# Waits of TensorE attached to other matmuls, fold and projection directly behind the pair sums, gathers one step further ahead

## The chip, the cores and the metric

The kernel runs on one core of one Trainium2 chip. The metric is device time in microseconds (us), here the median of three runs. TensorE multiplies matrices and writes to PSUM; VectorE, ScalarE and GpSimd work on elements (GpSimd on SBUF alone); each has its own queue, and the queues meet only at semaphores. In the profile PE is TensorE's matmul, PEld its weight load, DVE is VectorE, ACT ScalarE, POOL GpSimd and SP the queue that starts plain DMAs.

## The reference

Sixteen embedding tables are looked up for 2048 samples, which gives `e` of 16 fields by 256. Three layers of a field interaction follow, each with a weight of 16 by 256, then a small network of three matrices:

```python
    e = jnp.stack([tbl_0[ids[:, 0]], ...], axis=1)          # (2048, 16, 256)
    for i in range(n_layers):                                # 3
        z = jnp.einsum('bfe,bge->bfge', x, xk).reshape(B_, F_ * F_, E_)
        z = jnp.swapaxes(z, 1, 2)
        z = jnp.einsum('bcl,oc->bol', z, Ws[i]) + bs[i][None, :, None]
        z = jax.nn.relu(z)
        z = jnp.sum(z, axis=-1)
        outs.append(z)
        xk = jnp.broadcast_to(z[:, :, None], (B_, F_, E_))
    ...
    h = jnp.concatenate([z, dense_ctx], axis=1)              # 48 + 16
    h = jnp.maximum(h @ W_top1 + b_top1, 0.0)
    h = jnp.maximum(h @ W_top2 + b_top2, 0.0)
    y = h @ W_top3
```

Layer 0 multiplies every pair of fields element by element. In layers 1 and 2 the second factor is the same number over all elements, so the kernel projects `e` once and multiplies by it.

## The kernel before

**Tiling.** Eight samples of sixteen fields fill the 128 partitions. Two such tiles are one step; there are 128 steps (`STEPS`), and eight steps make a group `g` of 128 samples (16 groups). All engines walk through *slots* 0 to 159. In slot k each engine does its part of step k, or of a step a little ahead, and whatever piece of layers 1 and 2 or of the network the constants at the top put there (`ROUNDS`, `FOLD`, `PROJ`, and so on, as offsets to 8g).

**A step.** GpSimd gathers the rows of step k (two indirect DMAs, L257, into a ring `emb` of `EMB_RING` = 6), `LEAD` + 1 steps ahead of the product that it then makes. TensorE *transposes* them in slot k-2 (`turn`, L483, four matmuls with 128x128 weights into one of two halves of `turn_ps`). ScalarE copies them to `emb_t` (L398, L399). VectorE (L217), GpSimd (L217 and L267) and ScalarE (squares, L406) multiply the pairs into `prods`, a ring of three. TensorE then *sums the pairs* (`sum_pairs`, L503): 16 matmuls, in which four column strips of the array, 128 rows by 32 columns each, work side by side; they appear as 32 in the trace, since each f32 matmul is two passes. They go to the single buffer `sum_ps`, which ScalarE reads (`relu_pairs`, L416 and L419) before the next step's sums may start.

**Layers 1 and 2.** A *projection* (`project`, L546) per group, also with 128x32 strips. *Rounds* (`outer_round`, L531 and L535), four per layer and group, with 32x128 strips, into the single buffer `outer_ps`, which ScalarE reads (L426). There is one in slots 14 to 17, in every slot from 22 to 141, and in 146 to 149. A *fold* (`fold`, L555) per layer and group, with 128x32 strips again, which sums over one field: in slots 8g+18 and 8g+30. Projection, folds and both hidden layers (`hidden1` L563, `hidden2` L572) share the single buffer `wide_ps`; `wait_wide` waits for the reader of the one before. Small matmuls (`side`: L514, L517, L521) share a bank with the sums; `wait_side` waits for their readers.

**Order.** It is written out by hand. TensorE's loop over slots is `turn(slot + 2)`, a side matmul, `sum_pairs(slot)`, a round, and last the wide piece (projection, fold or hidden layer). GpSimd's loop, from slot -1, is a gather, `half_shift(slot + 1)`, a gather, `last_blocks(slot + 1)`, after `2 * LEAD` gathers in a row. An instruction holds one wait; further ones stand as separate waiting instructions before it in the queue. On TensorE the wait is on the weight load, and all waits of a block stand before its first matmul.

## Time and profile before

| | us |
|---|---|
| median of three runs | 630.85 (630.07 to 631.62) |
| profiled execution, whole | 628.34 |
| its span | 626.6 |
| TensorE busy (matmul) | 575.6 (92%) |
| VectorE busy | 499.5 (80%) |
| GpSimd busy | 463.7 (74%) |
| ScalarE busy | 455.3 (73%) |

The span runs from the first instruction to the last. Matmul times overlap, since one starts while the one before still drains, so the text measures TensorE from the start of one block to the start of the next. Slots 0 to 127 carry sums and end near 562 us; the rest of the span is the tail, in which only rounds, folds, hidden layers and small matmuls are left. The granted clock is the share of TensorE's 2.4 GHz that the chip gave; 0.50 is 1.2 GHz.

### The profile page before, as it was taken

The page shows a single profiled execution, that of the slowest core. Times are in us where ns is not written, and L with a number is a line of the kernel's source. Part 1 is how long each engine was busy: PE and PEld are TensorE (multiplying, and loading weights), DVE is VectorE, ACT ScalarE, POOL GpSimd, SP SyncE. Part 2 cuts the span into 40 slices and gives each one's busy share as a digit, 9 for nine tenths or more (in the row PEclk, how much of TensorE's full clock was granted, in tenths as well). Part 3 has the DMA queues.
Part 4 walks back from the last instruction along what each step waited for, and adds up shares of the span by engine and source line. Part 5 has one row for each costly group of instructions (what it writes and reads, how often), then busy time and mean ns, then how long its engine had stood idle before and what let it go on. Part 6 is the DMA issues. An engine that isn't in the chain of part 4 may idle for free.

```text
span 626.6 us, 19391 instructions
## 1 busy us (share of the span) xinstructions
PE 575.6 (92%) x7936; PEld 328.8 (52%) x7936; DVE 499.5 (80%) x220; ACT 455.3 (73%) x1298; POOL 463.7 (74%) x565
## 2 busy tenths in 40 slices
PE   2878798999999999999999999999999999997776
PEld 1444454555646555564656555565556555554354
DVE  5999999999898988889898988889888888941000
ACT  2666777787878787877887787777878788765542
POOL 6999999999988788888888888788878787621000
PEclk9999999999999999999999999999999999999988
DMA  3322222222222212222212122212212222100000
GB/s 97 112 73 73 69 70 68 70 70 65 69 64 61 61 58 63 61 61 62 65 56 65 57 61 60 69 55 68 60 55 67 61 61 57 47 3 1 1 1 2
DMA packets 14794, 35.97 MB, mean 57 GB/s; under 512 B 5922, under 2 KB 6306, under 8 KB 14690
## 3 DMA queue, kind: packets, MB, share of 16 engines
q0 software_dynamic: 12288, 33.57, 18.8%
q1 hardware_dynamic: 2418, 1.16, 0.7%
q8 instruction: 64, 1.05, 0.7%
q14 instruction: 24, 0.19, 0.1%
HBM read 34.70 MB, written 0.01 MB: 55 GB/s over the span
## 4 chain that ended last, share of the span: by engine, by line
PE 82%; POOL 8%; issue 4%; ACT 3%; DMA 1%; DVE 1%; SPq 0%; POOLq 0%
PE sum_ps L503 35%; PE turn_ps L483 10%; PE wide_ps L555 10%; PE outer_ps L535 8%; PE wide_ps L572 6%; PE wide_ps L546 4%; POOL emb L257 4%; PE outer_ps L531 4%; PE wide_ps L563 3%; POOL prods L267 2%; POOL prods L217 2%; ACT relu_k L426 1%; PE sum_ps L521 1%; PE sum_ps L517 1%; DVE prods L217 1%
## 5 line engine op out<-in xcount | busy, mean ns | idle before, releaser
L217 DVE TENSOR_TENSOR prods<-turn_ps,emb_t 128x3360 f32<-128x3360 f32 x128 | 466.1, 3655 | 55.1 <-ACT emb_t L399 52.2
L257 POOL DMA_INDIRECT emb<-tables,rows_sb x256 | 252.2, 985 | 45.4 <-issue 34.5
L503 PE MATMUL sum_ps<-prods,w_sb 128*32 128x272 f32 x4096 | 265.0, 397 | 18.6 <-POOL prods L217 11.1
L503 PEld LDWEIGHTS sum_ps<-prods,w_sb 128*32 128x32 f32 x4096 | 136.4, 110 | 103.6 <-issue 39.6
L426 ACT ACTIVATE relu_k<-outer_ps 128x1024 f32<-128x1024 f32 x128 | 132.4, 1035 | 11.2 <-PE outer_ps L535 11.1
L416 ACT ACTIVATE relu<-sum_ps,bias_sb 128x120 f32<-128x120 f32 x256 | 90.6, 361 | 58.4 <-PE sum_ps L503 57.2
L267 POOL TENSOR_TENSOR prods<-emb_t 128x256 f32<-128x256 f32 x128 | 95.3, 745 | 46.3 <-ACT emb_t L399 45.1
L398 ACT COPY emb_t<-turn_ps 128x512 f32<-128x512 f32 x128 | 75.3, 589 | 71.3 <-PE turn_ps L483 71.3
L483 PE MATMUL turn_ps<-ident_sb,emb 128*128 128x128 f32 x512 | 84.6, 289 | 12.7 <-DMA emb<-tables,rows_sb 10.0
L483 PEld LDWEIGHTS turn_ps<-ident_sb,emb 128*128 128x128 f32 x512 | 55.1, 142 | 60.5 <-issue 57.6
L406 ACT ACTIVATE prods<-emb_t 128x512 f32<-128x512 f32 x128 | 81.5, 637 | 3.3
L217 POOL TENSOR_TENSOR prods<-emb_t 128x224 f32<-128x224 f32 x128 | 77.5, 605 | 2.3
L535 PE MATMUL outer_ps<-proj_b,z_wide 32*128 32x256 f32 x1024 | 78.0, 378 | 0.0
L555 PE MATMUL wide_ps<-relu_k,fold_sb 128*32 128x256 f32 x1024 | 61.9, 382 | 1.5 <-ACT h L453 1.4
L291 POOL TENSOR_TENSOR z_wide<-z_cat,sample_sb 128x512 f32<-128x512 f32 x32 | 33.7, 1052 | 29.0 <-PE outer_ps L535 21.1
L369 DVE TENSOR_REDUCE z_cat<-wide_ps 128x16 f32<-128x256 f32 x32 | 13.4, 419 | 50.3 <-PE wide_ps L555 50.3
L416 ACT ACTIVATION_READ_ACCUMULATOR relu<-sum_ps,bias_sb 128x1 f32 x256 | 51.5, 201 | 0.0
L399 ACT COPY emb_t<-turn_ps 128x256 f32<-128x256 f32 x128 | 49.5, 386 | 0.0
L531 PE MATMUL outer_ps<-bias_wide,ones_sb 32*128 32x256 bf16 x512 | 37.0, 279 | 10.7 <-ACT relu_k L426 10.5
L531 PEld LDWEIGHTS outer_ps<-bias_wide,ones_sb 32*128 32x128 bf16 x512 | 12.9, 91 | 64.0 <-issue 52.7
L555 PEld LDWEIGHTS wide_ps<-relu_k,fold_sb 128*32 128x32 f32 x1024 | 30.3, 109 | 28.1 <-issue 9.3
L535 PEld LDWEIGHTS outer_ps<-proj_b,z_wide 32*128 32x128 f32 x1024 | 40.2, 186 | 0.0
(41 smaller groups left out, 284.3 us busy)
## 6 DMA issues: line engine op xcount, KB each, us to landing
emb<-tables,rows_sb POOLq DMA_INDIRECT x256
w_sb<-w_top SPq DMA_DIRECT2D x1, 512.0 KB, 4.3
ids_sb<-ids_t SPq DMA_DIRECT2D x1, 128.0 KB, 2.1
h<-dense_t SPq DMA_DIRECT2D x1, 128.0 KB, 2.9
w_sb<-w_top SPq DMA_DIRECT2D x1, 128.0 KB, 3.1
ident_sb<-ident SPq DMA_DIRECT2D x1, 64.0 KB, 2.1
w_sb<-w_cols SPq DMA_DIRECT2D x1, 64.0 KB, 1.9
wp_sb<-w_proj SPq DMA_DIRECT2D x1, 32.0 KB
```

Of the source, the lines that this page charges most:

```text
L217: eng.tensor_tensor(out, every, shifted, ALU.mult).then_inc(done, 1)
L257: nc.gpsimd.indirect_dma_start(out=emb[:, k % EMB_RING, t * E:(t + 1) * E], out_offset=None, in_=tables, in_offset=bass.IndirectOffsetOnAx ...
L267: nc.gpsimd.tensor_tensor(prod_blocks(k)[:, :, SHIFTS * F:], x[:, :, 0:SHIFTS], x[:, :, SHIFTS:F], ALU.mult).then_inc(prods_pool, 1)
L398: nc.scalar.copy(out[:, :, 0:F], src).then_inc(emb_t_ready, 1)
L406: nc.scalar.square(prod_blocks(k)[:, :, 0:F], emb_blocks(k)[:, :, 0:F]).then_inc(squares_ready, 1)
L416: nc.scalar.activation(relu0[:, t, :], sum_ps[:, t * PAIRS + F:(t + 1) * PAIRS], ACT.Relu, bias=bias_sb[:, 0:1], accum_out=pair_sum[:, g % ...
L426: nc.scalar.activation(relu_k[:, k, q, :, :], outer_ps[:, :, 0:F * F], ACT.Relu).then_inc(outer_relu, 1)
L483: last = nc.tensor.transpose(turn_ps[:, k % 2, i * P:(i + 1) * P], emb[:, k % EMB_RING, i * P:(i + 1) * P], ident_sb[:])
L503: last = nc.tensor.matmul(sum_ps[s * 2 * F:(s + 1) * 2 * F, 0:SUM_COLS], w_sb[:, c, odd, :], x[:, c, 2 * s + odd, :, :], start=c == 0 and ...
L531: nc.tensor.matmul(outer_ps[:, j, 0:F * F], ones_sb[j * R:(j + 1) * R, :], bias_wide[j * R:(j + 1) * R, k, :], start=True, stop=False)
L535: last = nc.tensor.matmul(outer_ps[:, j, 0:F * F], z_wide[j * R:(j + 1) * R, k, q, :], y[j * R:(j + 1) * R, k, :, :], start=False, stop=True)
L555: last = nc.tensor.matmul(wide_ps[j * R:(j + 1) * R, 0:F * F], fold_sb[:], relu_k[:, k, q, j, :], start=q == 0, stop=q == G4 - 1)
```

## The change

It does six things.

- `EMB_RING` goes from 6 to 8 and `LEAD` from 3 to 4: eight gathers stand before GpSimd's loop in place of six.
- The semaphores `prods_pool` and `squares_ready` are replaced by one per buffer of `prods` (`prods_other`, three increments per use), so that the sums wait for one.
- TensorE's waits go to other matmuls. The wait for a step's gather moves from its transposition into the sums of three steps before; the wait for ScalarE's reading of the sums goes to the fourth transposition of the slot, the one for a side matmul's reader to the third; `wait_wide` goes to the last of the 16 sums; the first round of four has its three waits on three matmuls. The wait for `emb_t_ready` in `turn` and that for `prods_dve` in the sums are left out, and so are the waits ahead of a side matmul for the readers of its bank, as the transpositions' waits stand before them.
- Projection and folds stand directly behind the sums, ahead of the slot's round. Hidden layers stay behind it.
- The last two steps (`STEPS - 2` on), which have no transposition beside them, keep their waits in front.
- ScalarE's `take_turned` waits for `sums_done` in place of two semaphores of products.

```diff
-EMB_RING = 6
+EMB_RING = 8
...
-LEAD = 3
+LEAD = 4
...
-        prods_pool = sem("prods_pool")
-        squares_ready = sem("squares_ready")
+        prods_other = [sem(f"prods_other{j}") for j in range(PRODS_RING)]
...
-                    at_least(act, prods_dve, old + 1)
-                    at_least(act, prods_pool, 2 * (old + 1))
+                    at_least(act, sums_done, old + 1)
...
             def turn(k):
 
                 if k < STEPS:
-                    pe.wait_ge(gathered[k % EMB_RING], PAIR * 16 * (k // EMB_RING + 1))
-                    at_least(pe, emb_t_ready, 2 * (k - 1))
+                    if k < 2:
+                        wait_gathered(k)
                     at_least(pe, prods_dve, k - 1)
                     for i in range(PAIR * EC):
+                        if i == 2 and k - 3 in SIDE_AT:
+                            wait_side(pe, k - 3)
+                        if i == 3:
+                            wait_sums_read(k - 2)
...
             def sum_pairs(k):
 
                 if k < STEPS:
-                    pe.wait_ge(squares_ready, k + 1)
-                    pe.wait_ge(prods_dve, k + 1)
-                    pe.wait_ge(prods_pool, 2 * (k + 1))
-                    wait_sums_read(k)
-                    wait_side(pe, k - 1)
+                    if k >= STEPS - 2:
+                        pe.wait_ge(prods_dve, k + 1)
+                        wait_side(pe, k - 1)
+                        wait_sums_read(k)
+                    pe.wait_ge(prods_other[k % PRODS_RING], N_OTHER * (k // PRODS_RING + 1))
...
+                                if (c, odd, s) == (1, 1, 2):
+                                    wait_gathered(k + 3)
+                                if (c, odd, s) == (1, 1, 3) and k in WIDE_AT and WIDE_AT[k][0] != "hidden2":
+                                    wait_wide(pe, *WIDE_AT[k])
...
             def outer_round(k, g, q):
 
-                if q == 0:
-                    pe.wait_ge(z_wide_ready[k], g + 1)
-                    pe.wait_ge(proj_ready, g + 1)
                 at_least(pe, outer_relu, ROUND_NO[k, g, q])
                 for j in range(J):
+                    if q == 0 and j == 1:
+                        pe.wait_ge(proj_ready, g + 1)
+                    if q == 0 and j == 2:
+                        pe.wait_ge(z_wide_ready[k], g + 1)
...
                 sum_pairs(slot)
+                if slot >= STEPS and slot in WIDE_AT:
+                    wait_wide(pe, *WIDE_AT[slot])
+                by_32 = slot in WIDE_AT and WIDE_AT[slot][0] in ("proj", "fold0", "fold1")
+                if by_32:
+                    wide(*WIDE_AT[slot])
                 if slot in ROUND_AT:
                     outer_round(*ROUND_AT[slot])
-                if slot in WIDE_AT:
+                if slot in WIDE_AT and not by_32:
                     wide(*WIDE_AT[slot])
```

TensorE in slot 30, before: L503 are the sums, L531 and L535 the round, L555 the fold, L483 the next transpositions.

```order
L503 MATMUL sum_ps<-prods,w_sb 32x272 [waits relu0_ready,prods_pool,z0_taken,prods_dve,squares_ready]
L503 MATMUL sum_ps<-prods,w_sb 32x272 x15
L531 MATMUL outer_ps<-bias_wide,ones_sb 128x256 [waits outer_relu,proj_ready,z_wide_ready0]
L531 MATMUL outer_ps<-bias_wide,ones_sb 128x256 x3
L535 MATMUL outer_ps<-proj_b,z_wide 128x256 x4
L555 MATMUL wide_ps<-relu_k,fold_sb 32x256 [waits outer_relu,z_ready0]
L555 MATMUL wide_ps<-relu_k,fold_sb 32x256 x15
L483 MATMUL turn_ps<-ident_sb,emb 128x128 [waits prods_dve,emb_t_ready,gathered3]
```

And TensorE in the same slot after the change, where L516 are the sums, L570 the fold, L546 and L550 the round and L496 the transpositions:

```order
L516 MATMUL sum_ps<-prods,w_sb 32x272 [waits prods_other0]
L516 MATMUL sum_ps<-prods,w_sb 32x272 x13
L516 MATMUL sum_ps<-prods,w_sb 32x272 [waits gathered1]
L516 MATMUL sum_ps<-prods,w_sb 32x272 [waits z_ready0]
L570 MATMUL wide_ps<-relu_k,fold_sb 32x256 [waits outer_relu]
L570 MATMUL wide_ps<-relu_k,fold_sb 32x256 x15
L546 MATMUL outer_ps<-bias_wide,ones_sb 128x256 [waits outer_relu]
L546 MATMUL outer_ps<-bias_wide,ones_sb 128x256 [waits proj_ready]
L546 MATMUL outer_ps<-bias_wide,ones_sb 128x256 [waits z_wide_ready0]
L546 MATMUL outer_ps<-bias_wide,ones_sb 128x256
L550 MATMUL outer_ps<-proj_b,z_wide 128x256 x4
L496 MATMUL turn_ps<-ident_sb,emb 128x128 [waits prods_dve]
```

The fold has moved from behind the round to between the sums and the round, and each waiting matmul has one wait.

TensorE in the tail, slot 138 and the round of slot 139, before:

```order
L531 MATMUL outer_ps<-bias_wide,ones_sb 128x256 [waits outer_relu,proj_ready,z_wide_ready1]
L531 MATMUL outer_ps<-bias_wide,ones_sb 128x256 x3
L535 MATMUL outer_ps<-proj_b,z_wide 128x256 x4
L555 MATMUL wide_ps<-relu_k,fold_sb 32x256 [waits outer_relu,z_ready1]
L555 MATMUL wide_ps<-relu_k,fold_sb 32x256 x15
L531 MATMUL outer_ps<-bias_wide,ones_sb 128x256 [waits outer_relu]
```

And TensorE there after the change, where L570 is the fold and L546 and L550 the rounds:

```order
L570 MATMUL wide_ps<-relu_k,fold_sb 32x256 [waits outer_relu,z_ready1]
L570 MATMUL wide_ps<-relu_k,fold_sb 32x256 x15
L546 MATMUL outer_ps<-bias_wide,ones_sb 128x256 [waits outer_relu]
L546 MATMUL outer_ps<-bias_wide,ones_sb 128x256 [waits proj_ready]
L546 MATMUL outer_ps<-bias_wide,ones_sb 128x256 [waits z_wide_ready1]
L546 MATMUL outer_ps<-bias_wide,ones_sb 128x256
L550 MATMUL outer_ps<-proj_b,z_wide 128x256 x4
L546 MATMUL outer_ps<-bias_wide,ones_sb 128x256 [waits outer_relu]
```

Two rounds now follow each other with no fold between them; the fold stands ahead of both.

GpSimd's queue at its start, as one difference (L267 and L217 are its products):

```order
 L248 MEMSET ones_sb 128x128
-L257 DMA emb<-tables,rows_sb 128x256 x7
+L257 DMA emb<-tables,rows_sb 128x256 x9
 L267 ISA
 L267 TENSOR_TENSOR prods<-emb_t 128x32x8
```

Two more gathers stand ahead of its first product.

## Rows read from the trace of the kernel before

**Rows 1.** The page's part 4: the chain that ended last, its shares by line

```profile
PE sum_ps L503 35%; PE turn_ps L483 10%; PE wide_ps L555 10%; PE outer_ps L535 8%; PE wide_ps L572 6%; PE wide_ps L546 4%; POOL emb L257 4%; PE outer_ps L531 4%; PE wide_ps L563 3%; POOL prods L267 2%; POOL prods L217 2%; ACT relu_k L426 1%; PE sum_ps L521 1%; PE sum_ps L517 1%; DVE prods L217 1%
```

**Rows 2.** Timeline, around slot 66; columns: start us, length us, engine, line, instruction

```profile
282.43 3.66 DVE L217 TENSOR_TENSOR prods<-turn_ps,emb_t 128x3360 f32<-128x3360 f32 x1
...
288.94 0.66 PE L483 MATMUL turn_ps<-ident_sb,emb 128*128 128x128 f32 x4
...
289.68 2.04 PE L503 MATMUL sum_ps<-prods,w_sb 128*32 128x272 f32 x32
...
291.65 0.29 PE L531 MATMUL outer_ps<-bias_wide,ones_sb 32*128 32x256 bf16 x4
...
292.31 1.93 PE L555 MATMUL wide_ps<-relu_k,fold_sb 128*32 128x256 f32 x32
...
294.17 0.66 PE L483 MATMUL turn_ps<-ident_sb,emb 128*128 128x128 f32 x4
```

**Rows 3.** Timeline, slot 66: four weight loads, ScalarE's last reading, the fourth transposition

```profile
288.94 0.42 PEld L483 LDWEIGHTS turn_ps<-ident_sb,emb 128*128 128x128 f32 x4 [0.33 <-issue]
...
289.11 0.29 ACT L419 ACTIVATE own<-sum_ps,bias_sb 128x32 f32<-128x32 f32 x1
...
289.33 0.27 PE L483 MATMUL turn_ps<-ident_sb,emb 128*128 128x128 f32 x1
```

**Rows 4.** Timeline of TensorE, slots 8 and 9 and slot 18

```profile
48.91 0.66 PE L483 MATMUL turn_ps<-ident_sb,emb 128*128 128x128 f32 x4
49.49 0.44 PE L503 MATMUL sum_ps<-prods,w_sb 128*32 128x272 f32 x4
...
84.39 2.04 PE L503 MATMUL sum_ps<-prods,w_sb 128*32 128x272 f32 x32
86.22 1.94 PE L555 MATMUL wide_ps<-relu_k,fold_sb 128*32 128x256 f32 x32
```

**Rows 5.** GpSimd: two early gathers, and its group from 12.95 to 106.6 us

```profile
9.47 0.95 POOL L257 DMA_INDIRECT emb<-tables,rows_sb  x1 [0.30 <-issue]
...
10.72 0.94 POOL L257 DMA_INDIRECT emb<-tables,rows_sb  x1 [0.30 <-issue]
...
L257 POOL DMA_INDIRECT emb<-tables,rows_sb x49 | 48.3, 986 | 7.8 <-issue 7.1 <-PE sum_ps L503 0.3 <-PE turn_ps L483 0.3
```

**Rows 6.** Timeline, slot 24: GpSimd's product and the sums behind it

```profile
106.00 0.60 POOL L217 TENSOR_TENSOR prods<-emb_t 128x224 f32<-128x224 f32 x1
...
106.81 0.44 PE L503 MATMUL sum_ps<-prods,w_sb 128*32 128x272 f32 x4 [0.40 <-POOL prods L217]
```

**Rows 7.** Timeline of the tail, rounds, folds and one reading by ScalarE

```profile
562.66 0.29 PE L531 MATMUL outer_ps<-bias_wide,ones_sb 32*128 32x256 bf16 x4
...
567.75 0.29 PE L531 MATMUL outer_ps<-bias_wide,ones_sb 32*128 32x256 bf16 x4
...
569.71 0.29 PE L531 MATMUL outer_ps<-bias_wide,ones_sb 32*128 32x256 bf16 x4 [1.24 <-ACT relu_k L426]
...
572.57 0.29 PE L531 MATMUL outer_ps<-bias_wide,ones_sb 32*128 32x256 bf16 x4
...
573.37 1.02 ACT L426 ACTIVATE relu_k<-outer_ps 128x1024 f32<-128x1024 f32 x1 [0.52 <-PE outer_ps L535]
574.45 0.29 PE L531 MATMUL outer_ps<-bias_wide,ones_sb 32*128 32x256 bf16 x4 [1.15 <-ACT relu_k L426]
...
580.32 1.93 PE L555 MATMUL wide_ps<-relu_k,fold_sb 128*32 128x256 f32 x32
...
582.61 0.29 PE L531 MATMUL outer_ps<-bias_wide,ones_sb 32*128 32x256 bf16 x4
...
588.33 0.29 PE L531 MATMUL outer_ps<-bias_wide,ones_sb 32*128 32x256 bf16 x4 [1.24 <-ACT relu_k L426]
...
590.86 0.29 PE L531 MATMUL outer_ps<-bias_wide,ones_sb 32*128 32x256 bf16 x4
```

**Rows 8.** Windows: us, busy us of five engines, granted clock, DMA share, GB/s

```profile
606.50:613.30 6.80, 6.30 (x35) 5.09 (x34) 0.00 (x0) 3.24 (x8) 0.00 (x0) 0.50 0.00 0
```

22 lines of the change are left out of this document (14 added, 8 removed).

## The prediction, made before the changed kernel had run

> **What bounds the kernel now.** I read the chain that ended last, then TensorE's timeline slot by slot, then GpSimd at the start and ScalarE in the last tenth. The chain lies for more than half of the span on three TensorE lines, the sums of pairs (35%), the transpositions and the fold [rows 1]. In the middle the slots repeat in groups of eight. VectorE is not the bound there: its product of slot 66 ends at 282.43+3.66 = 286.09, the sums that read it start at 289.68, 3.6 us later [rows 2]. So the middle is TensorE's own work and the steps between its blocks, with one exception. In an ordinary slot (transpositions, sums, one round) the transpositions start at 288.94 and the sums 0.74 us later [rows 2]; where nothing else holds them the same step takes 0.58 (48.91 to 49.49) [rows 4]. What holds them is ScalarE: it has read the slot before out of the one buffer of sums at 289.11+0.29 = 289.40, and the sums start 0.28 later, at 289.68 [rows 2, 3]. Such a slot comes three times in eight; I count 40 from slot 25 on. At the start GpSimd is the bound: from 12.95 to 106.6 us its instructions follow each other with only the issue gaps of the gathers between (49 gathers of 0.986 us, 7.8 us idle before them), and slot 24's sums start at 106.81, right behind its product, which ends at 106.60 [rows 5, 6]. In the tail, after slot 127, a round follows the one before only once ScalarE has read it: 572.57 to 574.45 = 1.88 us from round to round [rows 7].
>
> **The change part by part.**
>
> *Two more gathers ahead.* GpSimd issues eight gathers instead of six before its loop, one each 10.72-9.47 = 1.25 us [rows 5]: its first product comes 2.5 us later, and as it never stands still until slot 24, so does each one up to there. TensorE waits on it there, so nothing hides this. The wait itself gets shorter: today 0.21 us from the product's end to the sums (106.60 to 106.81) [rows 6], through two separate waits; after the change one wait on the weight load. The nearest row for such a wait is a round's: ScalarE ends at 573.37+1.02 = 574.39, the round starts at 574.45, 0.06 later [rows 7]; with 0.02 for the load in front of the matmul I take 0.08. Sum: +2.5-0.13 = **+2.4 us**. Bounds: 0, if TensorE makes it up later, and +2.5. TensorE cannot make it up, since from slot 25 on it has no idle time that GpSimd caused. The deeper ring of gathers removes no wait that I can find: the gathers of the steady part land slots before their use.
>
> *Fold and projection directly behind the sums.* Today a fold slot runs sums 289.68, round 291.65, fold 292.31, transpositions 294.17: steps of 1.97+0.66+1.86 = 4.49 us [rows 2]. The sums and the fold both use the array as four columns of 128 rows by 32, and where no round stood between them (slot 18) the fold started 86.22-84.39 = 1.83 us after the sums [rows 4], 0.14 to 0.15 less than a round does. The new slot is 1.83 (sums to fold), 1.86 (fold to round, taken as fold to transpositions) and 0.66 (round to transpositions, taken as round to fold) [rows 2, 4]: 4.35. One change of the array's shape goes per slot, 0.14 us. The projection uses the array as the fold does and trades the same changes of shape, so it is given the same 0.14. Such slots with sums and a round are 39 (slots 24, 26, 30, 32, 34 and so on to 126); the first is lost, since GpSimd still holds slot 26. 38 x 0.14 = **-5.3 us**. Bounds: 0 and 39 x 0.15 = -5.9; I take the timeline's. ScalarE then reads the round later and copies the transposed rows up to 0.6 us later; VectorE's 3.6 us hide that.
>
> *Waits spread out.* In long slots all waits are over before TensorE gets there, and a wait that is over costs nothing: the fold at 86.22 carries two and starts without a gap [rows 4]. So spreading them gains nothing, and the new waits inside a block, each on a load, cost nothing. In the 40 held slots the wait for ScalarE moves from the first sum to the fourth transposition. Today that transposition starts at 289.33 [rows 3], before ScalarE is done at 289.40; it will have to wait. Then: 0.04 to 0.06 from ScalarE's end to the load; 0.06 of the load exposed; 0.11 for the matmul (the four loads of 128x128 follow each other at about 0.11) [rows 3]; 0.09 for the change of shape. That is 0.30 to 0.32, against 0.28 today: what is saved in separate waits is paid again by a transposition that used to lie under the wait. 40 x 0.04 = **+1.6 us**. Bounds: if the wait vanished, 40 x (0.58-0.74) = -6.4; if the whole load (0.14) came on top, 0.08 more each, +4.8. I take the middle value, built from the nearest rows.
>
> A rule of the Trainium skill speaks the other way here (TensorE: Matmul & The Clock Gate, the section on packing small matmuls): a weight load overlaps a running matmul only if the two use different groups of rows. By it the fourth load would start only after the third matmul anyway, a held load would lose nothing, and the 1.6 would be near 0. Here four loads over all 128 rows are through in 0.42 us while the fourth matmul starts 0.39 us in [rows 3]: they overlap, so the trace does not agree, and I keep 1.6.
>
> *The tail.* Behind slot 127 there are no sums, and the new order hurts. The fold that stood behind a round ran while ScalarE read that round; now the fold has to wait for the round before it, and the next round is read with nothing beside it. Fold to round is 1.86 and round to round 1.88, 3.74 together. Slot 130: today round 130 to 131 is 572.57-569.71 = 2.86, so +0.88. Slot 134, where the fold starts at 580.32 either way (it waits for the second hidden layer): 582.61-580.32 = 2.29, so +1.45. Slot 138: 590.86-588.33 = 2.53, so +1.21. Against it slot 128, whose projection now fills ScalarE's reading of round 127: round 127 to round 129 is 567.75-562.66 = 5.09 today and 0.66+1.86+1.88 = 4.40 then, -0.69 [rows 7]. Sum **+2.8 us**; between +2.4 and +2.9, as the rows are rounded and the first loss partly meets the gain.
>
> Sum: +2.4-5.3+1.6+2.8 = +1.5 us. The profiled execution took 628.34 us (span 626.6, 1.7 around it); it would be 629.8. The median of the runs is 630.85, so I forecast 632.3. A measurement of this kernel can tell about 0.3%, 1.9 us: 629.0 to 632.7 is no change.
>
> **The rivals.**
>
> *The wait on ScalarE no longer shows (faster).* If waiting instructions, not ScalarE's reading, make the 0.74, the sums come at 0.58 in the 40 slots: -6.4 in place of +1.6, so 624.3. For it: two separate waits sit before those sums. Against it: the step is 0.58 in every slot in which ScalarE was done earlier, with the same waits. Chance 0.1.
>
> *The start hides (about no change).* If the clock or the first slots leave GpSimd room, the 2.4 go: 629.9. Against it: its filled stretch [rows 5]. Chance 0.1.
>
> *The clock falls in the thinner tail (slower).* From 606.5 to 613.3 the granted clock was 0.50 (1.2 GHz instead of 2.4), with 6.30 of 6.80 us busy [rows 8]; before it TensorE had done single rounds with waits between. The change makes two more such stretches, behind the folds of slots 130 and 134. Where blocks then run at half speed, half of the busy time is extra, up to 3.1 us; some of it lies under ScalarE, so 1.3 to 3: 633.6 to 635.3. It decides as soon as one stretch falls. Chance 0.25.
>
> *The held transposition costs its whole load (slower).* 40 x 0.12 = 4.8 instead of 1.6: 635.5. Chance 0.1.
>
> **How the numbers follow.** The forecast itself keeps 0.45. It stands 0.4 us below the upper bound of no change, so 0.07 of it fall beyond, and 0.03 below 629.0. Faster: 0.1 of the first rival, 0.02 of the second, 0.03: 0.15. Slower: 0.25, 0.1 and 0.07: 0.42. Same: 0.35 of the forecast and 0.08 of the second rival: 0.43. The range leaves out the first rival and reaches over the two slow ones, whose times have bounds of their own: 627.0 to 636.0.
>
> **What would show it.** In the profile after: the start of slot 24's sums at about 109.2 us; a fold slot of 4.35 us from sums to transpositions in place of 4.49, with sums to fold 1.83; in the held slots transpositions to sums still 0.75 or more, with the fourth transposition waiting on ScalarE's last reading; round to round 1.88 behind the folds of slots 130, 134 and 138; one or more stretches at half the clock behind 570 us. It is wrong if the step from transpositions to sums shrinks to 0.58 in the held slots, if slot 24 comes at 107, or if TensorE waits for a gather or for the fold's reader inside a block.

## The result: slower by 3.8%, and the profile after

| | us |
|---|---|
| before, median of 4 runs | 630.80 (630.07 to 631.62) |
| after, median of 4 runs | 654.84 (653.27 to 657.13) |
| ratio | 1.0384 (95% interval 1.0349 to 1.0418) |
| profiled execution after, whole | 654.38 |
| its span | 652.6 (before 626.6) |

The forecast was 632.3, the range 627.0 to 636.0. The three stages, cut at the sums of slots 24 and 126, show where the 26.0 us of the two spans are. First the windows view of the kernel before; columns are start and end, length, busy time of each engine with instructions, granted clock, DMA share, GB/s:

```profile
0.00:106.81 106.81, 77.59 (x1017) 43.68 (x1017) 98.08 (x45) 66.80 (x208) 92.20 (x116) 1.00 0.29 80
106.81:555.91 449.10, 446.17 (x6282) 252.79 (x6282) 397.54 (x167) 356.60 (x1025) 367.89 (x446) 1.00 0.21 61
555.91:626.60 70.69, 51.84 (x639) 32.30 (x638) 3.92 (x10) 31.94 (x66) 3.57 (x4) 0.93 0.00 1
```

The same view of the kernel after, at its own slots 24 and 126, with one stretch out of the tail, and one out of the start:

```profile
0.00:111.19 111.19, 81.69 (x1016) 40.67 (x1017) 97.13 (x45) 68.13 (x208) 94.98 (x119) 0.98 0.29 80
111.19:566.05 454.86, 448.43 (x6283) 253.47 (x6283) 396.90 (x167) 361.56 (x1025) 363.39 (x443) 1.00 0.21 59
566.05:652.60 86.55, 62.71 (x639) 39.68 (x638) 3.91 (x10) 31.86 (x66) 3.57 (x4) 0.76 0.00 1
584.34:594.58 10.24, 8.22 (x48) 6.36 (x48) 0.00 (x0) 3.79 (x8) 1.04 (x1) 0.50 0.00 0
...
24.55:27.97 3.42, 3.42 (x29) 1.53 (x33) 2.05 (x1) 1.49 (x3) 3.06 (x5) 0.50 0.28 77
```

The start is 4.4 us longer, the body (24 to 126) 5.8, the tail 15.9. The body was to get shorter. A *held slot*, below, is one whose sums have to wait for ScalarE. The tail does the same 639 matmuls, but its mean clock is 0.76 in place of 0.93.

**The body.** Timeline of the kernel after around slot 66, the answer to [rows 2] and [rows 3]:

```profile
295.31 0.20 PEld L496 LDWEIGHTS turn_ps<-ident_sb,emb 128*128 128x128 f32 x2 [0.33 <-issue]
...
295.48 0.28 ACT L419 ACTIVATE own<-sum_ps,bias_sb 128x32 f32<-128x32 f32 x1
295.64 0.25 ACT L436 COPY h<-sum_ps 48x128 f32<-48x128 f32 x1
295.95 0.20 PEld L496 LDWEIGHTS turn_ps<-ident_sb,emb 128*128 128x128 f32 x2 [0.44 <-issue]
295.95 0.44 PE L496 MATMUL turn_ps<-ident_sb,emb 128*128 128x128 f32 x2 [0.20 <-issue]
...
296.32 2.04 PE L516 MATMUL sum_ps<-prods,w_sb 128*32 128x272 f32 x32
...
298.18 1.91 PE L570 MATMUL wide_ps<-relu_k,fold_sb 128*32 128x256 f32 x32
300.02 0.29 PE L546 MATMUL outer_ps<-bias_wide,ones_sb 32*128 32x256 bf16 x4
...
300.67 0.66 PE L496 MATMUL turn_ps<-ident_sb,emb 128*128 128x128 f32 x4
```

The fold moved as forecast: sums to transpositions 300.67-296.32 = 4.35 us (before 4.49). But the step in front of it, transpositions to sums, is 296.32-295.31 = 1.01 where it was 0.74. The loads stop after two transpositions. The third does not wait for L419, which ends at 295.48+0.28 = 295.76, but for the copy behind it, L436, the reader of the side matmul: it ends at 295.64+0.25 = 295.89, and the load starts at 295.95. Before, that same copy stood behind L419, and the sums waited for it as well:

```profile
289.28 0.25 ACT L436 COPY h<-sum_ps 48x128 f32<-48x128 f32 x1
...
289.65 0.19 PEld L503 LDWEIGHTS sum_ps<-prods,w_sb 128*32 128x32 f32 x8 [0.29 <-issue]
```

It ended at 289.28+0.25 = 289.53, and that, not 289.40, was what held the sums. The waits view of the kernel after, from 111 to 566 us, counts these places; columns: engine, waiting line, who was waited for, us in total, times, longest:

```profile
PEld turn_ps L496 <- ACT y_sb L439: 4.9, 11, 0.4
PEld turn_ps L496 <- ACT h L436: 4.8, 11, 0.4
PEld turn_ps L496 <- ACT z_cat L433: 4.4, 12, 0.4
```

**The tail.** The kernel before around its slots 131 to 134; L563 and L572 are the hidden layers:

```profile
575.10 1.16 PE L563 MATMUL wide_ps<-h,w_sb 64*128 64x128 f32 x8
576.32 0.29 PE L531 MATMUL outer_ps<-bias_wide,ones_sb 32*128 32x256 bf16 x4
...
577.59 2.02 PE L572 MATMUL wide_ps<-h,w_sb 128*128 128x128 f32 x16 [0.53 <-ACT h L447]
579.54 0.29 PE L531 MATMUL outer_ps<-bias_wide,ones_sb 32*128 32x256 bf16 x4
```

And after, where L578 and L587 are the hidden layers and L570 the fold:

```profile
584.84 0.40 PE L546 MATMUL outer_ps<-bias_wide,ones_sb 32*128 32x256 bf16 x4 [1.24 <-ACT relu_k L426]
585.00 1.09 PE L550 MATMUL outer_ps<-proj_b,z_wide 32*128 32x256 f32 x8
586.02 2.07 PE L578 MATMUL wide_ps<-h,w_sb 64*128 64x128 f32 x8
589.33 0.40 PE L546 MATMUL outer_ps<-bias_wide,ones_sb 32*128 32x256 bf16 x4 [1.23 <-ACT h L447]
...
590.51 3.78 PE L587 MATMUL wide_ps<-h,w_sb 128*128 128x128 f32 x16
595.00 1.93 PE L570 MATMUL wide_ps<-relu_k,fold_sb 128*32 128x256 f32 x32 [0.71 <-ACT h L453]
```

Two things are to be seen. The round at 589.33 now waits for `h L447`, the reader of the first hidden layer; before, it ran while ScalarE read. And every block from 584.84 to 594 takes about twice its time (3.78 us for 2.02): the granted clock is 0.50. Such stretches make up 41 us of the tail after, 10 us before.

### The profile page after: what moved, and what is told of

It is laid out like the page before. It is cut to its first block, busy times and chain, and to the rows that moved or that the text cites. A ratio compares the mean times of both kernels' runs of the same rounds, so it can differ in the third digit from the quotient of the medians.

```text
span 652.6 us, 18768 instructions
## 1 busy us (share of the span) xinstructions
PE 592.8 (91%) x7936; PEld 333.8 (51%) x7936; DVE 497.9 (76%) x220; ACT 461.5 (71%) x1298; POOL 461.9 (71%) x565
## 4 chain that ended last, share of the span: by engine, by line
PE 83%; ACT 11%; issue 4%; another core or an unknown queue 1%; DMA 1%; POOL 0%; DVE 0%; SPq 0%; ACTq 0%
PE sum_ps L516 39%; PE turn_ps L496 10%; PE wide_ps L570 9%; PE outer_ps L550 7%; PE wide_ps L587 6%; ACT relu L416 5%; PE wide_ps L561 4%; PE outer_ps L546 3%; PE wide_ps L578 3%; ACT relu_k L426 2%; ACT own L419 1%; PE sum_ps L535 1%; PE sum_ps L531 1%; ACT h L447 1%
## 5 line engine op out<-in xcount | busy, mean ns | idle before, releaser
L217 DVE TENSOR_TENSOR prods<-turn_ps,emb_t 128x3360 f32<-128x3360 f32 x128 | 464.8, 3651 | 66.8 <-ACT emb_t L399 51.9
L516 PE MATMUL sum_ps<-prods,w_sb 128*32 128x272 f32 x4096 | 267.8, 399 | 2.4 <-issue 2.4
L516 PEld LDWEIGHTS sum_ps<-prods,w_sb 128*32 128x32 f32 x4096 | 126.8, 110 | 95.1 <-issue 19.2
L267 POOL TENSOR_TENSOR prods<-emb_t 128x256 f32<-128x256 f32 x128 | 95.0, 742 | 57.7 <-ACT emb_t L399 53.0
L496 PE MATMUL turn_ps<-ident_sb,emb 128*128 128x128 f32 x512 | 97.9, 296 | 33.5 <-ACT own L419 11.5
L496 PEld LDWEIGHTS turn_ps<-ident_sb,emb 128*128 128x128 f32 x512 | 55.1, 142 | 86.3 <-issue 47.3
L550 PE MATMUL outer_ps<-proj_b,z_wide 32*128 32x256 f32 x1024 | 80.8, 390 | 0.0
L217 POOL TENSOR_TENSOR prods<-emb_t 128x224 f32<-128x224 f32 x128 | 77.1, 602 | 2.4
L570 PE MATMUL wide_ps<-relu_k,fold_sb 128*32 128x256 f32 x1024 | 64.5, 387 | 4.6 <-ACT relu_k L426 2.5
L570 PEld LDWEIGHTS wide_ps<-relu_k,fold_sb 128*32 128x32 f32 x1024 | 37.8, 112 | 25.3 <-issue 4.8
L546 PEld LDWEIGHTS outer_ps<-bias_wide,ones_sb 32*128 32x128 bf16 x512 | 13.0, 91 | 73.6 <-issue 59.6
L546 PE MATMUL outer_ps<-bias_wide,ones_sb 32*128 32x256 bf16 x512 | 37.6, 284 | 13.8 <-ACT relu_k L426 10.1
L550 PEld LDWEIGHTS outer_ps<-proj_b,z_wide 32*128 32x128 f32 x1024 | 41.5, 192 | 0.0
```

What stands on the lines that cost most here:

```text
L217: eng.tensor_tensor(out, every, shifted, ALU.mult).then_inc(done, 1)
L267: nc.gpsimd.tensor_tensor(prod_blocks(k)[:, :, SHIFTS * F:], x[:, :, 0:SHIFTS], x[:, :, SHIFTS:F], ALU.mult).then_inc(prods_other[k % PROD ...
L496: last = nc.tensor.transpose(turn_ps[:, k % 2, i * P:(i + 1) * P], emb[:, k % EMB_RING, i * P:(i + 1) * P], ident_sb[:])
L516: last = nc.tensor.matmul(sum_ps[s * 2 * F:(s + 1) * 2 * F, 0:SUM_COLS], w_sb[:, c, odd, :], x[:, c, 2 * s + odd, :, :], start=c == 0 and ...
L546: nc.tensor.matmul(outer_ps[:, j, 0:F * F], ones_sb[j * R:(j + 1) * R, :], bias_wide[j * R:(j + 1) * R, k, :], start=True, stop=False)
L550: last = nc.tensor.matmul(outer_ps[:, j, 0:F * F], z_wide[j * R:(j + 1) * R, k, q, :], y[j * R:(j + 1) * R, k, :, :], start=False, stop=True)
```

## The experiments

Each run's verdict is its ratio to the kernel before on the same chip, with the 95% interval. This table has, from one profile of each, the start of slot 24's sums, the time from there to slot 126's (the body), from there to the end (the tail), and the tail's granted clock.

| run | median us | ratio (95%) | slot 24 | body | tail | clock |
|---|---|---|---|---|---|---|
| before | 630.80 | | 106.81 | 449.10 | 70.7 | 0.93 |
| after | 654.84 | 1.0384 (1.0349 to 1.0418) | 111.19 | 454.86 | 86.5 | 0.76 |
| after_again | 647.19 | 1.0279 (1.0247 to 1.0311) | 108.93 | 455.94 | 80.5 | 0.84 |
| lead4 | 632.26 | 1.0035 (1.0009 to 1.0061) | 109.28 | 450.80 | 72.7 | 0.87 |
| fold_mid | 625.17 | 0.9929 (0.9904 to 0.9954) | 106.80 | 446.14 | 71.7 | 0.89 |
| tail_old | 637.29 | 1.0132 (1.0111 to 1.0153) | 109.15 | 456.20 | 68.1 | 0.96 |
| waits_front | 638.87 | 1.0142 (1.009 to 1.0194) | 108.96 | 442.96 | 84.0 | 0.81 |
| side_front | 627.83 | 0.9997 (0.9976 to 1.0019) | 108.95 | 447.24 | 69.9 | 0.93 |
| relu_front | 635.32 | 1.0126 (1.0079 to 1.0173) | 109.04 | 454.61 | 69.9 | 0.95 |
| tail_fold | 638.30 | 1.0193 (1.0146 to 1.0241) | 106.72 | 449.18 | 77.8 | 0.84 |
| tail_h1 | 632.72 | 1.0106 (1.0052 to 1.0161) | 106.46 | 448.93 | 74.4 | 0.91 |
| tail_both | 638.13 | 1.0209 (1.0143 to 1.0274) | 106.62 | 449.11 | 80.6 | 0.84 |
| after_fill | 640.74 | 1.0215 (1.0167 to 1.0264) | 108.93 | 454.87 | 76.5 | 0.93 |
| one_sem | 627.02 | 0.999 (0.9967 to 1.0012) | 106.42 | 448.09 | 71.8 | 0.89 |
| side_first | 625.63 | 0.9934 (0.9914 to 0.9955) | 106.77 | 446.78 | 74.5 | 0.86 |
| front_old | 620.81 | 0.99 (0.9866 to 0.9934) | 106.51 | 441.83 | 68.0 | 0.96 |
| wide_back | 619.88 | 0.9868 (0.9847 to 0.989) | 106.58 | 440.19 | 71.5 | 0.89 |
| front_fill | 617.21 | 0.9843 (0.9801 to 0.9885) | 106.47 | 441.84 | 67.0 | 1.00 |
| best_fill | 615.56 | 0.9808 (0.9792 to 0.9824) | 106.48 | 440.24 | 67.1 | 1.00 |

### The parts of the change, one at a time

**lead4**: the kernel before with eight gathers ahead.

```diff
-EMB_RING = 6
+EMB_RING = 8
-LEAD = 3
+LEAD = 4
```

> The kernel before with LEAD 4 and a ring of 8 alone. If each of GpSimd's early products comes 2.5 us later and TensorE waits on them (my step): slot 24's sums at about 109.3 us in place of 106.81, and the whole run 2.4 us longer, ratio 1.004. If the start hides it: below 0.5 us, ratio 1.000. If the later start also keeps TensorE's clock at half for longer: up to 4 us, and the first slots show doubled sums.

Slot 24 came 2.5 us later, and the whole takes 0.35% longer. The term of the start is confirmed. The deeper ring gave nothing back in the body; that is 1.7 us longer as well (450.8 against 449.1): 0.65 in slots 27 to 29, 0.44 in slot 35, most of the rest 0.04 to 0.13 in one held slot of each group. The same part shows between waits_front and front_old, which below slot 128 differ in the gathers alone: 443.0 and 441.8. No run shows what it comes from. With six gathers ahead the body repeats from profile to profile (448.9 to 449.2 in four with this code); with eight, that of the kernel after took 454.86, 454.87, 455.94 and 456.20.

**fold_mid**: the kernel before with projection and folds ahead of the round up to slot 127.

```diff
+                by_32 = slot < STEPS and slot in WIDE_AT and WIDE_AT[slot][0] in ("proj", "fold0", "fold1")
+                if by_32:
+                    wide(*WIDE_AT[slot])
                 if slot in ROUND_AT:
                     outer_round(*ROUND_AT[slot])
-                if slot in WIDE_AT:
+                if slot in WIDE_AT and not by_32:
```

> The kernel before with projection and folds ahead of the round in slots below 128 alone; the tail keeps its order. If a change of the array's shape costs 0.14 us and nothing gives it back: a group of eight slots of 35.1 us in place of 35.5 and 5.3 to 5.5 us less in all, ratio 0.9915. Rival, ScalarE's reading of the later round delays the transposed rows and gives it back: group of 35.5 or more, ratio 1.00 or above.

Faster by 0.7%, 4.0 to 4.5 us against the forecast's 5.3. From slot 30 each slot with such a piece is 0.14 us shorter. The body gained 3.0 in the profile: in most groups one held slot is 0.08 to 0.11 longer than before, and slots 27 to 29, still held by GpSimd, gave back 0.8. I put the first down to ScalarE, which reads the round later; no run tests that, and in front_old (below) it is gone.

**tail_old**: the kernel after with the old order and the old place of the waits from slot 128 on.

```diff
-                if slot >= STEPS and slot in WIDE_AT:
-                    wait_wide(pe, *WIDE_AT[slot])
-                by_32 = slot in WIDE_AT and WIDE_AT[slot][0] in ("proj", "fold0", "fold1")
+                by_32 = slot < STEPS and slot in WIDE_AT and WIDE_AT[slot][0] in ("proj", "fold0", "fold1")
...
                 if slot in WIDE_AT and not by_32:
+                    if slot >= STEPS:
+                        wait_wide(pe, *WIDE_AT[slot])
                     wide(*WIDE_AT[slot])
```

> The changed kernel with the old order and the old places of the waits in slots 128 and up. The trace of after puts 652.6 - 566.05 = 86.6 us behind slot 126's sums, that of before 626.6 - 555.91 = 70.7. If the tail's order is the cause (fold ahead of the round, the round of slots 133, 141, 149 behind the reader of the first hidden layer, and the half clock that follows): 14 to 16 us less than after, about 640. If the half clock there comes from the body or by chance: less than 5 us back.

The tail is 68.1 us in place of 86.5, and the ratio came down from 1.0384 to 1.0132: all of the tail's loss hangs on those lines.

**waits_front**: the kernel after with the waits for ScalarE's reading and for the side reader in front of the sums again.

```diff
-                        if i == 2 and k - 3 in SIDE_AT:
-                            wait_side(pe, k - 3)
-                        if i == 3:
-                            wait_sums_read(k - 2)
...
+                    wait_side(pe, k - 1)
+                    wait_sums_read(k)
                     pe.wait_ge(prods_other[k % PRODS_RING], N_OTHER * (k // PRODS_RING + 1))
```

> The changed kernel with the waits for ScalarE's readings of the sums and of the side matmul back in front of the sums instead of on the third and fourth transposition. After has groups of eight slots of 36.0 us, before 35.5. If the transpositions held behind those waits are what the body loses (0.27 us in three slots of eight): groups of 35.1 to 35.2 and 12 to 13 groups x 0.85 = 10 to 11 us less, and the start gives back 1 to 2 more; about 643. If something else lengthens the groups: 36.0 stays.

The body fell by 11.9 us, to 443.0, which is 6.1 below the kernel before. The loss of the body is in these two waits. The whole came 4 us lower than expected.

### Which of the two waits

Both runs stand on tail_old. **side_front** takes back the side wait alone, **relu_front** the other alone (the lines that put them back in front of the sums are left out here):

```diff
 side_front
-                        if i == 2 and k - 3 in SIDE_AT:
-                            wait_side(pe, k - 3)
 relu_front
-                        if i == 3:
-                            wait_sums_read(k - 2)
```

> The changed kernel with the old order behind slot 127 (as in the run tail_old) and with the wait for a side matmul's reader back in front of the sums; the wait for ScalarE's reading of the sums stays on the fourth transposition. Per group of eight slots the run tail_old takes 36.08 us, and with both waits in front it is 34.98. Theory S: the side wait on the third transposition is what costs, as two transpositions and a change of shape then stand behind the reader that comes last: a group takes 35.1 or less, and the whole 625 or less. Theory R, the one of the prediction: ScalarE's reading is what holds the slot, and its wait on the fourth transposition costs; a group stays at 35.9 or more, 636 or more. Both about equally: 35.5, 631.

> The mirror of it: the changed kernel with the old order behind slot 127 and with the wait for ScalarE's reading of the sums back in front of the sums; the side wait stays on the third transposition. Theory S: nothing comes back, a group takes 36.0 us and the whole 636 to 638. Theory R: a group takes 35.1, the whole 625. Both about equally: 35.5, 631.

side_front: a group takes 35.39 us, and the whole 627.83. In the groups that repeat, tail_old takes 36.04 and waits_front 34.94; the 36.08 and 34.98 of the expectation are means with an odd slot in them. relu_front: 36.04, 635.32, nothing back to speak of. Between the theories: the side wait is worth 0.65 a group, 0.22 per held slot. The other costs 0.45 a group, but only where the side wait no longer hides it. Timeline of side_front, slot 66:

```profile
290.51 0.28 ACT L419 ACTIVATE own<-sum_ps,bias_sb 128x32 f32<-128x32 f32 x1
290.68 0.25 ACT L436 COPY h<-sum_ps 48x128 f32<-48x128 f32 x1
...
290.85 0.14 PEld L494 LDWEIGHTS turn_ps<-ident_sb,emb 128*128 128x128 f32 x1 [0.20 <-ACT own L419]
291.11 0.16 PEld L515 LDWEIGHTS sum_ps<-prods,w_sb 128*32 128x32 f32 x8
```

Here the fourth transposition waits for L419 (ends 290.79, load 290.85) as I had forecast for the change, and the sums follow 0.32 after L419. That is the figure that I had taken; but without any wait in the block they come 0.64 us after the transpositions' start (waits_front), not 0.76; that and the like in the two other held slots (0.65 for 0.79, 0.59 for 0.77) is the 0.45 a group.

### The tail: order or clock

Three edits of the kernel before, each from slot 128 on alone:

```diff
 tail_fold, and tail_both
+                by_32 = slot >= STEPS and slot in WIDE_AT and WIDE_AT[slot][0] in ("proj", "fold0", "fold1")
+                if by_32:
+                    wide(*WIDE_AT[slot])
                 if slot in ROUND_AT:
 tail_h1: hidden2 only; tail_both: every wide piece
+                if slot >= STEPS and slot in WIDE_AT and WIDE_AT[slot][0] == "hidden2":
+                    wait_wide(pe, *WIDE_AT[slot])
                 if slot in ROUND_AT:
```

> The kernel before, with projection and folds ahead of the round in slots from 128 on alone. Two theories of the 15.9 us that the changed kernel's tail (from slot 126's sums to the end) is longer. Theory O (order): waits that came onto the chain; this edit then costs my prediction's tail sum, +2.8 us: about 632.0 beside 629.2. Theory C (clock): the new gaps bring the granted clock down; then the half-clock stretches of the tail grow from 10 us to 25 us or more, and the time is 637 or more. If neither holds, it stays within 1 us of the kernel before.

> The kernel before, with the wait for the first hidden layer's reader put ahead of the round in slots 133, 141 and 149 (it stood behind the round, ahead of the second hidden layer). Theory O: the round starts about 1.3 us later in each of three slots, and the second hidden layer behind it, which had hidden the reader behind that round, by one round of 0.65 us or more: +2 to +4 us, 631 to 633. Theory C: the gap brings the clock down at each of these places, since the second hidden layer then runs at 3.8 instead of 2.0 us: 3 x 1.8 more, 636 to 639.

> The kernel before with the changed kernel's whole tail (slots from 128 on: projection and folds ahead of the round, every wait for the reader of the wide buffer ahead of the round). Start and body are those of before. If all of the tail's loss sits in these two edits, tail +15.9 us: 645. If the loss needs something of the body too (how warm the clock is when the tail starts), well under that: 635 to 640. If the two edits add up and the clock plays no part, the sum of the two single runs.

All three are slower. Where the clock was full in both kernels, the starts of the blocks give the cost of the order alone. In tail_fold the projection's place gave back 0.71 us, slot 130 cost 0.89, slot 134 1.45 and slot 138 1.21: +2.8, as forecast. In tail_h1 the two hidden layers stand 3.05 us apart in place of 2.49:

```profile
574.58 1.16 PE L563 MATMUL wide_ps<-h,w_sb 64*128 64x128 f32 x8
576.97 0.29 PE L531 MATMUL outer_ps<-bias_wide,ones_sb 32*128 32x256 bf16 x4 [1.23 <-ACT h L447]
...
577.63 2.05 PE L572 MATMUL wide_ps<-h,w_sb 128*128 128x128 f32 x16
```

That is 0.56 here and as much between the layers of slots 140 and 141; with a third such pair (148 and 149) +1.7. Order alone is +4.5. The tails grew by 7.1, 3.7 and 9.9 us; the rest, 4.3, 2.0 and 5.4, goes with longer half-clock stretches (25.5, 14.1 and 25.5 us, against 10.2 before). One profile is one execution, though, and the old tail too was at half clock for 5.8 (front_old) to 20.6 us (side_first), so tail_h1's 14.1 shows nothing by itself. The runs beside the profiles do: the mean clock of a whole run was 0.969 to 0.983 in tail_fold and tail_both and 0.980 to 0.991 in tail_h1, against 0.989 to 0.999 in the seven of the kernel before. Neither of my two theories holds alone. The tail of tail_both is that of after_again to 0.1 us at the same clock, 0.84: the two edits are the whole of the tail's change.

**after_fill** puts work in the gaps of the kernel after, and leaves its order as it is:

```diff
+                if slot >= STEPS and slot in ROUND_AT and slot not in WIDE_AT:
+                    for i in range(6):
+                        nc.tensor.transpose(turn_ps[:, i // 4, i % 4 * P:(i % 4 + 1) * P], ident_sb[:], ident_sb[:])
```

> The changed kernel, plus six transpositions of a constant matrix behind each round of the tail that has no wide piece behind it; nothing reads them, the outputs are unchanged. At full clock six take 0.66 us and lie in the 1.2 us in which TensorE waits for ScalarE, so they cost nothing themselves. Theory C: with TensorE busier the granted clock stays at full for most of the tail, and the blocks that ran at half speed (second hidden layer 3.8 instead of 2.0 us, first 2.1 instead of 1.2, and rounds and folds beside them) come back: 654.8 less 8 to 10, about 646. Theory O: the clock only follows the waits and is worth little: 654 or more.

More work in the tail made it shorter (the whole came 5 us lower than expected), by 10.0 us against the first profile of after and by 4.0 against the second (after_again, next). Its clock rose from 0.76 and 0.84 to 0.93, though 10.6 us of it were still at half clock, and the hidden layers of slots 140 and 141 run at their full speed:

```profile
606.33 1.16 PE L578 MATMUL wide_ps<-h,w_sb 64*128 64x128 f32 x8
608.72 0.29 PE L546 MATMUL outer_ps<-bias_wide,ones_sb 32*128 32x256 bf16 x4 [1.23 <-ACT h L447]
...
609.37 2.05 PE L587 MATMUL wide_ps<-h,w_sb 128*128 128x128 f32 x16
```

The wait for `h L447` is still there, and so is the 3.04 us between the layers; what went is the half speed. At the clock that the kernel before had (0.93), the changed tail costs 5.8 us, 1.3 over the 4.5 of the order. So of the first profile's 15.9 us 4.5 to 5.8 are order, and the rest, about two thirds, goes with the clock.

**after_again** is the kernel after, unchanged.

> The changed kernel once more, unchanged, for its start: in its first profile the granted clock fell to 0.50 from 24.55 to 27.97 us and slot 24 came at 111.19 us; after_fill, which has the same start, had no such fall and slot 24 at 108.93. If the fall at the start is part of the change, slot 24 comes at 111 again; if it is chance of one execution, at 108.9, and 2.3 us of the first profile's 26.0 are not the change's. The tail is expected as in the first profile, 83 to 87 us with more than 30 us of it at half clock.

Its slot 24 comes at 108.93, and its start has no fall of the clock; the windows view of the stretch in which the first profile had 0.50:

```profile
24.80:28.20 3.40, 2.79 (x44) 1.39 (x40) 3.40 (x2) 2.47 (x9) 3.07 (x4) 1.00 0.31 82
```

So 2.3 us of the first profile's 4.4 at the start belong to that execution, and 2.1 to the gathers. The fall of the clock is not all of the 2.3, and it did not come first. Timeline of the first profile:

```profile
23.49 0.36 ACT L416 ACTIVATE relu<-sum_ps,bias_sb 128x120 f32<-128x120 f32 x1 [6.20 <-remote]
...
24.52 0.47 PE L496 MATMUL turn_ps<-ident_sb,emb 128*128 128x128 f32 x1 [2.40 <-ACT own L419]
...
24.92 3.52 PE L516 MATMUL sum_ps<-prods,w_sb 128*32 128x272 f32 x32
```

And of after_again:

```profile
22.02 0.36 ACT L416 ACTIVATE relu<-sum_ps,bias_sb 128x120 f32<-128x120 f32 x1 [4.97 <-PE sum_ps L516]
...
23.30 2.04 PE L516 MATMUL sum_ps<-prods,w_sb 128*32 128x272 f32 x32
```

ScalarE's first reading of the sums began 1.5 us late, after something that the profile doesn't name ("remote"), and the held transposition behind it came at 24.52 for 23.04, just before the clock fell. Slot 1's sums then took 3.52 us in place of 2.04.

The tail of after_again, 80.5 us with 25.5 at half clock, was shorter than the 83 to 87 that I expected. The same program took 647 to 657 us in its six runs, with mean clocks from 0.980 to 0.962. Between the two profiles 15.5 us more of half clock (41.0 and 25.5) go with 6.0 us of tail, 0.39 per us. The Trainium skill (TensorE: Matmul & The Clock Gate, the section on HAM oscillation) counts half of the throttled time as lost, which would be 7.8 as an estimate; the trace is below that. In the stretch 584.34 to 594.58 TensorE was busy for 8.22 of 10.24 us, and half of the busy time is 0.40 per us, so the waits in these stretches explain the difference, as an estimate.

### What is left of the change

**front_old** takes the three losses out of the kernel after: `LEAD` 3, the waits of waits_front, the tail of tail_old.

> What is left of the change when its three losses are taken out: six gathers ahead as before, the waits for ScalarE's reading and for the side reader in front of the sums, the old order behind slot 127; projection and folds ahead of the round before slot 128, one semaphore per product buffer and the other waits inside the blocks stay. If the parts add up, slot 24 at 106.8, slot 126 443 us later at 549.8, and a tail of 68 to 71: a span of 618 to 621, 7 us below the kernel before (ratio about 0.989). If the eight gathers are needed by the wait for a gather inside the sums, TensorE stands there and the body gets longer than 443.

A ratio of 0.99: the parts add up, and two kinds of gain are in the body (441.8 against 449.1, so 7.3). One is the folds, 3.6. The other shows in held slots, 0.09 to 0.12 us each. Two runs on the kernel before ask what it is. **one_sem** joins the semaphores of the products (with ScalarE's `take_turned` waiting for `sums_done`, as in the change) and leaves out the sums' wait for `prods_dve`; the cut shows the sums:

```diff
-                    pe.wait_ge(squares_ready, k + 1)
-                    pe.wait_ge(prods_dve, k + 1)
-                    pe.wait_ge(prods_pool, 2 * (k + 1))
+                    if k >= STEPS - 2:
+                        pe.wait_ge(prods_dve, k + 1)
+                    pe.wait_ge(prods_other[k % PRODS_RING], 3 * (k // PRODS_RING + 1))
                     wait_sums_read(k)
                     wait_side(pe, k - 1)
```

> The kernel before, with the two semaphores of products joined into one per buffer, and the sums' wait for VectorE's product left out where the transpositions ahead of them have it: three waits in front of the sums in place of five, nothing else. My prediction took this part as worth nothing (waits that are over cost nothing), so 627.9 beside 627.9. The other theory, from the traces after: in the held slots the step from transpositions to sums is 0.64 us where three waits stand there and 0.74 where five do, so the waits behind the last one to come still have to be read one by one: 3 x 0.1 per group, 40 slots, 4 us less, ratio 0.994.

No measurable difference in the ratio; in its one profile the body is 1.0 us shorter (448.1), most of it 0.05 in one held slot of each group. **side_first** moves one line:

```diff
+                    wait_side(pe, k - 1)
                     pe.wait_ge(squares_ready, k + 1)
                     pe.wait_ge(prods_dve, k + 1)
                     pe.wait_ge(prods_pool, 2 * (k + 1))
                     wait_sums_read(k)
-                    wait_side(pe, k - 1)
```

> The kernel before, with one line moved: the wait for the side matmul's reader is written first of the five in front of the sums in place of last. The wait that is written first rides on the weight load itself; the others become separate instructions ahead of it. In before (and in one_sem, which brought nothing) the side wait, which comes last in the held slots, is a separate instruction, and the load starts 0.113 us after ScalarE's reading; in front_old it is on the load, 0.052 us after. If that is what front_old gained in the body beside the folds, a held slot takes 0.09 us less here, 3 x 15 of them 4 us less, ratio about 0.994. If the joined semaphore is needed too, no difference.

Faster by 0.66%, as expected. Of those 4 us (2.8 to 5.4 by the interval) the profile shows 2.3 in the body (446.8), 0.04 to 0.12 per held slot; the rest isn't placed. Timeline of side_first, slot 66; the copy ends at 289.18:

```profile
288.93 0.25 ACT L436 COPY h<-sum_ps 48x128 f32<-48x128 f32 x1
...
289.24 0.16 PEld L503 LDWEIGHTS sum_ps<-prods,w_sb 128*32 128x32 f32 x8 [0.28 <-ACT h L436]
```

The load starts 0.06 after the copy, in the kernel before 0.12 (289.53 to 289.65), and the first sum another 0.03 earlier behind its load. In the trace the wait that is written first rides on the load; the others stand as instructions of their own ahead of it. front_old happens to write the side wait first. Its 3.7 us beside the folds are about the 1.0 of one_sem and the 2.3 of side_first together.

**wide_back** is front_old with the wide buffer's wait on the fold instead of the last of the sixteen sums:

```diff
-                                if (c, odd, s) == (1, 1, 3) and k in WIDE_AT and WIDE_AT[k][0] != "hidden2":
-                                    wait_wide(pe, *WIDE_AT[k])
...
                 if by_32:
+                    wait_wide(pe, *WIDE_AT[slot])
                     wide(*WIDE_AT[slot])
```

> front_old with the wait for the wide buffer's reader back in front of the projection, fold or hidden layer; in front_old, as in the changed kernel, it stands on the last of the sixteen sums. In the slots of the second fold (70, 78 and so on) that sum waits for ScalarE's reading of the second hidden layer: the sums last 1.80 us instead of 1.65. Theory W: this eats the 0.14 us that the fold's new place gains there; with the wait on the fold 0.14 us come back in each of 12 groups, 1.7 us of 616.3 in the span. Theory N: the reader is what comes last either way, no difference.

The body is 1.6 us shorter (0.15 in each of the 11 such slots from 38 to 118). Timeline of front_old, slot 70, sums and round:

```profile
304.18 2.19 PE L512 MATMUL sum_ps<-prods,w_sb 128*32 128x272 f32 x32
...
308.04 0.29 PE L541 MATMUL outer_ps<-bias_wide,ones_sb 32*128 32x256 bf16 x4
```

And wide_back:

```profile
303.66 2.04 PE L510 MATMUL sum_ps<-prods,w_sb 128*32 128x272 f32 x32
305.52 1.91 PE L563 MATMUL wide_ps<-relu_k,fold_sb 128*32 128x256 f32 x32
307.36 0.29 PE L539 MATMUL outer_ps<-bias_wide,ones_sb 32*128 32x256 bf16 x4
```

Sums to round: 3.86 against 3.70. The last sum has no use for that buffer, but it waited for its reader. The ratio does not separate wide_back from front_old (0.9868 and 0.99, with overlapping intervals), since its tail happened to run at 0.89; the fillers settle that.

**front_fill** and **best_fill** are front_old and wide_back with the six fillers behind the tail's lone rounds, and behind the last group's z_t matmul and first hidden layer.

> front_old, plus six transpositions that nothing reads behind each round of the tail that has no wide piece behind it, and behind the last group's z_t matmul and first hidden layer. Clock theory: the half-clock stretches behind 600 us (7 to 12 us, mostly under the last group's layers, where the second hidden layer takes 2.6 to 3.3 instead of 1.8 us) shrink, and the tail comes to 66 to 68: 1 to 3 us below front_old. If the last stretch comes whatever TensorE does, no difference; if the fillers stand in the way of real blocks, up to 2 us above.

> front_fill with the same edit as wide_back: the version that takes every part that gained. If theory W holds, 1.7 us below front_fill's 617.2, at 615.5 (ratio to the kernel before about 0.981), with the granted clock at 1.0 to the end in every run and the runs within 0.3 us of each other, as in front_fill; if theory N holds, 617.2.

The clock is 1.000 in every run of both, and the runs agree within 0.12 us (615.51 to 615.63), where front_old's spread over 3.8. best_fill is 1.65 us below front_fill, and in the profiles its body is 1.60 shorter, which is the wide wait. Its tail:

```profile
546.72:613.80 67.08, 55.65 (x699) 35.05 (x698) 3.91 (x10) 32.05 (x66) 3.56 (x4) 1.00 0.01 1
```

It is faster than both kernels, by 1.9% and, by the two ratios (0.9808 / 1.0384), 5.5%.

## Why the prediction was wrong, point by point

**The gathers, +2.4.** Right for slot 24: 2.5 in lead4, 2.1 in after_again. That they would cost nothing in the body was not: 1.7 in lead4, 1.1 between front_old and waits_front, with the cause open.

**Fold and projection, -5.3.** The mechanism and the 0.14 us were right in each slot (fold_mid). Two steps failed. First, in the change 12 of the 38 slots (those of the second fold) gained nothing, for the wide wait had moved into the sums (wide_back); a wait for the fold's reader inside a block was one of the signs of being wrong that I had named. Second, I had written that spread waits cost nothing because they are over, and had looked only at the first fold's slots. That leaves about -3.6.

**The waits spread out, +1.6.** The step that failed is the name of the holder. I read L419 as the last reading before the held sums, as it is the last of `relu_pairs`; one row further stood L436, the side reader, which ends 0.13 us later. Held slots come three times in eight, as often as side matmuls; that should have sent me to it. The rival of the costlier held transposition (635.5) had the same wrong holder. Measured, a held slot costs 0.22 to 0.28, not 0.04; 36 of them 8.9 us (body +5.8 and folds -3.6 make 9.4, of which 0.4 lie in slots 25 to 29). The price of a wait on the fourth transposition alone was right (side_front: 0.32).

**The tail, +2.8.** The part of projection and folds was right (2.8). Missing was the round that waits for the first hidden layer's reader, +1.7; the order of the instructions showed that wait, and I had given it no price.

**The clock, a rival at 0.25.** The sum put this at nothing; it is the largest single miss. As a rival it was the right mechanism, too small: I gave it 1.3 to 3 us, from two more stretches of 6.8. The changed tail was at half clock for 25.5 and 41.0 us in the two profiles, 15 to 31 more than in that of before, and that was worth 5 to 11. [rows 8] had shown what such a stretch does to busy work; I had treated its length as fixed.

Of the first profile's 26.0 us: start 4.4 (2.1 gathers, 2.3 of that execution alone, a late first reading and a fall of the clock), body 5.8 (held slots about +9, folds about -3.5), tail 15.9 (order 4.5, the rest goes with the clock). The sum had 1.5. What it missed: the tail's clock 11.4, the held slots 7.5, that execution's start 2.3, the folds 1.8, the tail's order 1.7.

## What to carry over

Before a wait is moved onto an instruction, find the reader that really comes last, by its end in the trace and not by its place in the code, and count what then stands behind that reader. A wait written for an instruction that does not need it holds everything after it. Where a stage has small blocks with waits between, ask what the clock will do there: a few matmuls that nobody reads, laid in the gaps, gave back 4 to 10 us of the changed tail (after_fill) and 3.6 us of front_old (front_fill).

## What was not expected of the hardware

- The spread between runs goes with the clock. The spans of the kernel before went from 622.3 us at a mean clock of 0.999 to 628.2 at 0.985; with fillers and 1.000 four and five runs agree to 0.2 us.
- In the tail of after the clock fell although the longest idle time of TensorE ahead of it there was 1.24 us (before 584.84): rounds of 0.65 us every 1.9 us, and folds between them, were what it did before the fall. With six transpositions in the gaps it stayed up throughout in front_fill and best_fill, and fell for 10.6 us in after_fill.
- The end of a reading to the waiting load is 0.06 us when the wait is the load's own, and 0.12 when it is a separate instruction before the load. One line in the source chooses between them, worth 0.66% here (side_first, 0.45 to 0.86 by the interval).
- Open: why the same tail (tail_both, after, after_again, waits_front) gets between 25.5 and 41.0 us of half clock, and why the old one gets between 5.8 and 20.6. The start's clock fell in one profile of the kernel after, right behind 2.40 us in which TensorE waited for ScalarE; why ScalarE was late there is open too. Nothing here shows what sets it off in one execution and not in another.
